# Bucket-sort ranks in a graph-network kernel: one scan and one predicated copy per bucket, with bucket totals from ScalarE

## The reference, cut to what matters

```
edge_index = jnp.stack([src, dst])
h = jnp.maximum(_layernorm(x, axis=-1), 0.0)
x = x + _L0_gnn_ref(h, edge_index, edge_weight1, ...)   # attention, segment_sum over dst
x = x + _L1_gnn_ref(h, edge_index, ...)                 # three rounds, segment_sum over dst and src
x = x + _L2_gnn_ref(h, edge_attr_256, edge_index, ...)  # softmax over dst and src together
x = x + _L3_gnn_ref(h, edge_index, edge_weight, ...)    # segment_sum over dst
```

## Time and profile before

| | us |
|---|---|
| median of three runs | 6442.14 |
| lowest, highest | 6439.19, 6449.53 |
| the profiled execution's own time | 6450.52 |
| its span, first to last instruction | 6448.7 |
| VectorE busy (share of the span) | 3708.4 (58%) |
| GpSimd busy | 3098.7 (48%) |
| TensorE busy | 3350.8 (52%) |
| ScalarE busy | 1198.0 (19%) |

### The profile page before, as it was taken

One profiled execution on the slowest core, in us unless ns is written; L12 is line 12 of the kernel. 1 busy time (PEld: TensorE's weight loads), 2 busy tenths in 40 slices (PEclk: granted clock), 3 DMA queues, 4 the chain that ended last, 5 costly groups with the idle time before them and its releaser, 6 DMA issues. The chain is left out here.

```text
span 6448.7 us, 88107 instructions
## 1 busy us (share of the span) xinstructions
PE 3350.8 (52%) x20820; PEld 2500.4 (39%) x20821; DVE 3708.4 (58%) x13503; ACT 1198.0 (19%) x3916; POOL 3098.7 (48%) x3167
## 2 busy tenths in 40 slices
PE   1000110016662666356638877968964988942333
PEld 0000010004442555345525544545554777732333
DVE  9200830049994777667777437337354888875444
ACT  0000000005551111011100000000003988930000
POOL 2777177726761777367730550541571000005775
PEclk9999999988886555555558888878987999975555
DMA  7000000006662333243327677657742434401112
GB/s 291 3 3 3 22 3 3 3 12 175 191 185 85 78 77 77 28 84 78 77 45 134 140 156 136 151 131 144 170 110 59 114 100 119 114 23 47 49 50 45
DMA packets 942678, 567.18 MB, mean 88 GB/s; under 512 B 598770, under 2 KB 873436, under 8 KB 938460
## 3 DMA queue, kind: packets, MB, share of 16 engines
q1 hardware_dynamic: 841820, 405.86, 24.7%
q0 software_dynamic: 100608, 158.42, 11.6%
HBM read 384.62 MB, written 179.43 MB: 87 GB/s over the span
## 5 line engine op out<-in xcount | busy, mean ns | idle before, releaser
L796 POOL DMA_INDIRECT fild_g<-table,fild_ring x416 | 427.6, 1028 | 1102.5 <-ACT fild_ring L810 978.7
L235 POOL DMA_INDIRECT recordsS<-sortS_rS,sortS_addrS x416 | 425.4, 1023 | 262.9 <-DVE sortS_addrS L276 136.5
L796 POOL DMA_INDIRECT gatAp_g<-table_heads,gatAp_ring x416 | 429.3, 1032 | 246.3 <-issue 123.7
L796 POOL DMA_INDIRECT gatBp_g<-table_head,gatBp_ring x416 | 411.6, 990 | 237.8 <-issue 122.8
L235 POOL DMA_INDIRECT recordsD<-sortD_rD,sortD_addrD x392 | 401.1, 1023 | 221.8 <-issue 119.1
L860 PE MATMUL fild_ps<-fild_g,fild_oh 128*128 128x128 f32 x832 | 213.2, 438 | 396.0 <-DMA fild_g<-table,fild_ring 267.4
L756 PE MATMUL pairs_p_b<-pairs_blk,pairs_oh 128*128 128x256 f16 x1024 | 294.1, 313 | 177.0 <-DVE pairs_oh L743 134.7
L860 PEld LDWEIGHTS fild_ps<-fild_g,fild_oh 128*128 128x128 f32 x832 | 185.2, 327 | 423.9 <-DVE fild_oh L912 198.0
L154 POOL DMA_INDIRECT gcn0e_held_attr<-in_edge_attr,recD x184 | 178.8, 971 | 354.1 <-POOLq L86 262.2
L771 ACT CAST pairs_blk<-pairs_p_b 128x512 f16<-128x512 f32 x512 | 285.2, 587 | 219.0 <-PE pairs_p_b L758 160.8
L154 POOL DMA_INDIRECT gcn2e_held_attr<-in_edge_attr,indexS x184 | 178.9, 972 | 281.2 <-POOLq L86 189.5
(11 more groups left out here) (656 smaller groups left out, 10465.5 us busy)
## 6 DMA issues: line engine op xcount, KB each, us to landing
gcnw_strip<-pairs SPq DMA_DIRECT2D x150, 800.0 KB, 6.5
pairs<-pairs_blk SPq DMA_DIRECT2D x768, 64.0 KB
pairs<-sortD_blank SPq DMA_DIRECT2D x27, 1600.0 KB, 38.0
attD_g<-attrD SPq DMA_DIRECT2D x104, 256.0 KB, 3.6
attS_g<-attrS SPq DMA_DIRECT2D x104, 256.0 KB, 3.6
pairs<-pairs_blk POOLq DMA_DIRECT2D x256, 64.0 KB, 2.3
attrD<-pairs_held_attr SPq DMA_DIRECT2D x56, 256.0 KB, 2.5
gatAp_rowb<-locD SPq DMA_DIRECT2D x104, 128.0 KB, 3.0
```

The costliest lines, as they stand in the source:

```text
L235: pool.indirect_dma_start(self.rec_dram, bass.IndirectOffsetOnAxis(ap=self.addr[:, c:c + 1], axis=0), self.r[:, c, :], None, bounds_check= ...
L796: pool.indirect_dma_start(rows(u, k), None, table, bass.IndirectOffsetOnAxis(ap=ring[:, u, k:k + 1], axis=0)).then_inc(gathered[u], 16)
```

## The change

The bucket totals are made first. ScalarE copies each one-hot plane and sums it along the columns into `tot` (`totals`); TensorE adds these sums over the partitions with a matrix of ones (`p_tot`), between buckets 3 and 4; the seven small instructions follow at once. Then TensorE makes one row per bucket instead of two: two matmuls into the same PSUM buffer give the increment from one column's rank to the next, `before` of this column plus `after` (ones minus `before`) of the column ahead of it. VectorE sums that row along the columns, with the bucket's first slot as the starting value, and copies the result into `slot` where the plane is one. There are four PSUM buffers for the rows instead of two. One GpSimd instruction makes `after16`. The stages behind are the same.

```
+            link(nc.gpsimd.tensor_tensor(C.after16[:], C.ones[:], C.before[:], ALU.subtract))
...
-        self.p_w = [ph.ps(f"p_w{side}{q}", [P, 512]) for q in range(2)]
-        self.p_t = [ph.ps(f"p_t{side}{q}", [P, 512]) for q in range(2)]
+        self.p_w = [ph.ps(f"p_w{side}{q}", [P, 512]) for q in range(4)]
+        self.p_tot = ph.ps("p_tot" + side, [P, NT])
+        self.junk = sb("junk", [P, 2, ncol], BF16)
...
+    def totals(self, act):
+        for b in range(NT):
+            act.wait_ge(self.oh_made, b + 1)
+            if b >= 2:
+                act.wait_ge(self.totalled, b - 1)
+            self.nc.scalar.activation(self.junk[:, b % 2], self.ohb[:, b, :], ACT.Copy,
+                                      accum_out=self.tot[:, b:b + 1]).then_inc(self.totalled, 1)
+
     def rank(self, V, dve):
...
+        dve.wait_ge(self.summed_up, 1)
+        V.ts(self.first[:], self.p_tot[:], float(P - 1), ALU.add)
...
         for b in range(NT):
             dve.wait_ge(self.ranked, b + 1)
-            V.link(nc.vector.tensor_tensor_scan(self.cum[:, 1:n + 1], self.p_t[b % 2][:, 0:n], self.zero[:], 0.0, ALU.add, ALU.add))
-            nc.vector.tensor_copy(self.tot[:, b:b + 1], self.cum[:, n:n + 1])
-            nc.vector.tensor_tensor(self.tmp[:], self.cum[:, 0:n], self.p_w[b % 2][:, 0:n], ALU.add).then_inc(self.taken, 1)
+            nc.vector.tensor_tensor_scan(self.cum[:, 0:n], self.p_w[b % 4][:, 0:n], self.zero[:],
+                                         self.first128[:, b:b + 1], ALU.add, ALU.add).then_inc(self.taken, 1)
             dve.wait_ge(self.taken, b + 1)
-            V.tt(self.tmp[:], self.tmp[:], self.ohb[:, b, :], ALU.mult)
-            V.tt(self.slot[:], self.slot[:], self.tmp[:], ALU.add)
...
-        for b in range(NT):
-            V.stt(self.slot[:], self.ohb[:, b, :], self.first128[:, b:b + 1], self.slot[:], ALU.mult, ALU.add)
+            V.link(nc.vector.copy_predicated(self.slot[:], self.ohb[:, b, :].bitcast(dt.uint16), self.cum[:, 0:n]))
...
             pe.wait_ge(self.oh_made, b + 1)
-            if b >= 2:
-                pe.wait_ge(self.taken, b - 1)
-            nc.tensor.matmul(self.p_w[b % 2][:, 0:n], self.C.before16[:], self.ohb[:, b, :], start=True, stop=True)
-            nc.tensor.matmul(self.p_t[b % 2][:, 0:n], self.C.ones16[:], self.ohb[:, b, :], start=True, stop=True).then_inc(self.ranked, 1)
+            if b == 4:
+                pe.wait_ge(self.totalled, NT)
+                nc.tensor.matmul(self.p_tot[:], self.C.ones[:], self.tot[:], start=True, stop=True).then_inc(self.summed_up, 1)
+            if b >= 4:
+                pe.wait_ge(self.taken, b - 3)
+            nc.tensor.matmul(self.p_w[b % 4][:, 0:n], self.C.before16[:], self.ohb[:, b, :], start=True, stop=False)
+            nc.tensor.matmul(self.p_w[b % 4][:, 1:n], self.C.after16[:], self.ohb[:, b, 0:n - 1], start=False,
+                             stop=True).then_inc(self.ranked, 1)
...
+        @block.scalar
+        def _(act):
+            j.totals(act)
```

More of the change, by code:

```diff
@@ L205, in __init__ @@
         self.first = sb("first", [P, NT])
+        self.tiles = sb("tiles", [P, NT])
         self.first128 = sb("first128", [P, NT])
-        self.p_w = [ph.ps(f"p_w{side}{q}", [P, 512]) for q in range(2)]
-        self.p_t = [ph.ps(f"p_t{side}{q}", [P, 512]) for q in range(2)]
+        self.p_w = [ph.ps(f"p_w{side}{q}", [P, 512]) for q in range(4)]
+        self.p_tot = ph.ps("p_tot" + side, [P, NT])
+        self.junk = sb("junk", [P, 2, ncol], BF16)
+        self.totalled, self.summed_up = ph.sem("totalled" + side), ph.sem("summed_up" + side)
         self.p_cnt = ph.ps("p_cnt" + side, [P, NT])
@@ L250, in rank @@
             nc.vector.tensor_scalar(self.ohb[:, b, :], self.bucketf[:], float(b), None, ALU.is_equal).then_inc(self.oh_made, 1)
+        dve.wait_ge(self.summed_up, 1)
+        V.ts(self.first[:], self.p_tot[:], float(P - 1), ALU.add)
+        V.link(nc.vector.tensor_copy(self.toti[:], self.first[:]))
+        V.link(nc.vector.tensor_single_scalar(self.toti[:], self.toti[:], P.bit_length() - 1, ALU.logical_shift_right))
+        V.link(nc.vector.tensor_copy(self.tiles[:], self.toti[:]))
+        V.link(nc.vector.tensor_tensor_scan(self.first[:], self.tiles[:], self.zero[:, 0:NT], 0.0, ALU.add, ALU.add))
@@ L251, in rank @@
+        V.tt(self.first[:], self.first[:], self.tiles[:], ALU.subtract)
+        V.ts(self.first128[:], self.first[:], float(P), ALU.mult)
         for b in range(NT):
             dve.wait_ge(self.ranked, b + 1)
-            V.link(nc.vector.tensor_tensor_scan(self.cum[:, 1:n + 1], self.p_t[b % 2][:, 0:n], self.zero[:], 0.0, ALU.add, ALU.add))
-            nc.vector.tensor_copy(self.tot[:, b:b + 1], self.cum[:, n:n + 1])
-            nc.vector.tensor_tensor(self.tmp[:], self.cum[:, 0:n], self.p_w[b % 2][:, 0:n], ALU.add).then_inc(self.taken, 1)
+            nc.vector.tensor_tensor_scan(self.cum[:, 0:n], self.p_w[b % 4][:, 0:n], self.zero[:],
+                                         self.first128[:, b:b + 1], ALU.add, ALU.add).then_inc(self.taken, 1)
@@ L263, in rank @@
-        V.link(nc.vector.tensor_tensor_scan(self.first[:], self.tot[:], self.zero[:, 0:NT], 0.0, ALU.add, ALU.add))
-        V.tt(self.first[:], self.first[:], self.tot[:], ALU.subtract)
-        V.ts(self.first128[:], self.first[:], float(P), ALU.mult)
-        for b in range(NT):
-            V.stt(self.slot[:], self.ohb[:, b, :], self.first128[:, b:b + 1], self.slot[:], ALU.mult, ALU.add)
+            V.link(nc.vector.copy_predicated(self.slot[:], self.ohb[:, b, :].bitcast(dt.uint16), self.cum[:, 0:n]))
@@ L2217, in program @@
         C.before16 = sb("before16", [P, P], BF16)
+        C.after16 = sb("after16", [P, P], BF16)
         C.ext_col = sb("ext_col", [1, NE], I32)
```

## The result

After the change the kernel takes 6435.18 us (median of 17 runs, 6430.63 to 6441.06), beside 6446.54 for the kernel before in the same comparison: a ratio of 0.9984 (95% interval 0.9976 to 0.9991). That is a gain of 11 us where 71 were forecast. The profile after was taken on an execution with a span of 6439.2 us.

A forecast was written before the change was run, and what follows sets the result against it. VectorE's ranking followed by GpSimd's scatters, twice, was taken to bound the sorts. Gains of 34.1 us in D and 36.9 in S, less 0.4, made 71: 6371 us against 6442.1, with 6354 to 6394 holding about 8 in 10.

The forecast's parts named there:

- A microsecond off the ranking should therefore be one off the kernel.: Both sorts: GpSimd's scatters wait for VectorE's ranking, 89.80 us in D and 93.57 in S, so its savings carry through whole.
- The passes behind `addr` are unchanged and move with it.: Behind each sort's address cast: the passes keep their length and start earlier by the gain; no cost counted.
- The sum: Whole kernel: 34.1 us gained in D plus 36.9 in S, less 0.4 for constants, 71 us rounded.
- the sign to look for: Stages behind the sorts: one that runs longer than before would show what the sum left out.
- The bucket loop: VectorE's 25 buckets per sort: 1.71 us each in D and 1.79 in S, together 42.7 and 44.7 us.
- The totals: ScalarE's 25 plane sums per sort, ahead of VectorE's loop: 0.63 us each in D, 0.65 in S.
- ScalarE's table load: Start of D's totals on ScalarE: 1.28 us charged to sort D, none in S.
- The overlap in that price: ScalarE's pitch per total: each copy in a row was taken to overlap its neighbour by about 0.07 us.
- ScalarE or VectorE: Place of the totals: VectorE alone would expose 14 us instead of 11, some 3 us a sort worse.
- The scatters beside the blank stores: GpSimd's earlier D scatters while blank stores fill the DMA engines: costed at nothing.
- The first rival: Sort D: scatters stand behind the blank stores, so D gains nothing and the kernel takes 6405; chance 8%.
- the other two: Sorts' ranking: predicated copy slow, 6461 at 2.4 us each, 3%; or ScalarE's totals so late nothing is gained, 6442, 2%.

The follow-up runs named there:

- run 6: Kernel after with 9 one-column memsets on VectorE in sort D behind the low compare, moving its later loops 8 instructions: 6364.89 us, ratio 0.9881.
- run 9: Kernel after with each bucket's predicated copy replaced by multiplication and addition, the rest of the change kept, loops lying well: 6396.23 us.
- run 7: Kernel after with all 25 bucket totals reduced by VectorE and none summed by ScalarE, no memsets: 6382.17 us.
- run 8: Kernel after with ScalarE summing 18 bucket totals and VectorE reducing 7, no memsets: 6356.89 us, ratio 0.9870.
- run 2: Kernel after with 129 one-column memsets on VectorE in sort D behind the low compare, moving its later loops 128 instructions: 6436.60 us.
- run 4: Kernel after with 24 memsets on GpSimd ahead of sort D's scatters to start them later, VectorE's program untouched: 6487.33 us.

## Why the prediction was wrong

**The step that failed** is the end of the first paragraph: "A microsecond off the ranking should therefore be one off the kernel." It puts everything behind the ranking at nothing, as does "The passes behind `addr` are unchanged and move with it." The code of the later stages is unchanged and the barriers do carry a gain on, but VectorE's program for them had moved by 198 instructions. Of the 78 us that the sorts gained, the attention D loop took back 66 and gather B 6. The sum had no term for it, the rivals no case, and no row of the kernel before showed a loop that pays. The text did name the sign to look for, a later stage that runs longer.

**The sum itself stood.** With the loops lying well the kernel takes 6364.89 (run 6) where 6371 was forecast, inside the range; the gain is 80 us beside 71. Point by point:
- *The bucket loop*: forecast 42.7 and 44.7 us; in D from 39.01 to 81.50, 42.5. The scan's start value costs 0.06 as the earlier trace rows had it (1.03 against 0.97), the predicated copy with the 16-bit mask 0.60 as taken from the 32-bit one, and run 9 confirms what it is worth.
- *The totals* were mis-sized: 0.51 us each, not 0.63, since reading out a sum (0.18) lies beside the next pass. Over 25 that is 3 us a sort. ScalarE's table load, charged to D with 1.28, came at 4.9 us while ScalarE was idle. Together they make the 4 us by which D beat its 34.1; S, with 40.2 against 36.9, had the 3 alone. The overlap in that price was misread too: four copies overlap three times, so the row gives 0.10 us and not 0.07.
- *ScalarE or VectorE*: the forecast put VectorE-only some 3 us a sort behind, and in D it was 5.3 (run 7). The Trainium skill ("ScalarE: Activation LUTs", Rules for kernel authors) would give adds to VectorE. The traces agree only that a sum of a plane is a little shorter there, 0.47 against 0.51. But VectorE is the engine that the sort waits for, and in run 8, where each took a part, the sorts were done soonest.
- *The scatters beside the blank stores*: nothing, as costed. They start at 86.43, and their mean stayed 1023 ns. The first rival didn't happen, nor did the other two.

**Why the same stall costs 66 us in one loop and 6 in another.** After the change VectorE's waits on "issue" are 63.1 us in attention D and 55.7 us in gather B (of the first line here, a wait for gathered rows, there were 128.7 us before):

```profile
DVE gatBp_z L1016 <- DMA gatBp_g<-table_head,gatBp_ring: 84.6, 58, 4.6
DVE gatBp_msg L1051 <- issue: 29.6, 10, 3.4
DVE gatB_acc L1040 <- issue: 26.1, 12, 2.7
```

In gather B VectorE waits for gathered rows anyway, and the stall comes out of that wait: 44 us of it went. GpSimd's 416 gathers set that pass, with 417.2 us of work and 118.8 of issue. Attention D has no such slack. Before, ScalarE was busy 321.3 us and TensorE 318.4 of its 352.5, and by the waits above both wait for VectorE's `attD_df` once it stands still. TensorE's clock falls after the stall (windows of the turn shown above: busy us of PE, PEld, DVE, ACT, POOL, then granted clock, DMA share, GB/s):

```profile
4941.00:4949.00 8.00, 4.25 (x34) 3.57 (x33) 1.48 (x7) 3.77 (x13) 0.00 (x0) 0.98 0.47 132
4949.00:4957.00 8.00, 5.34 (x31) 5.37 (x32) 6.06 (x35) 4.50 (x16) 0.00 (x0) 0.59 0.00 1
```

After eight microseconds in which TensorE was busy for 4.25, the granted clock is 0.59 of full, mostly the 1.2 GHz level instead of 2.4, and full again in the 23 us behind. What that adds to the price no run separates from the stall.

The Trainium skill ("Runtime: NRT & Kernel Launch", Instruction fetch mechanics) says that a taken branch whose target is no longer held forces a fetch before execution goes on; the traces agree, with 4 to 7 us a turn. It gives the blocks as 256 instructions, two of them held; here the measurements decide otherwise, since run 2, moved by 128, paid just as much.

## What to carry to other kernels

A change that adds or removes instructions moves every loop behind it on that engine, and here a loop of 274 instructions paid or not by where it began. So compare the length of every later stage before believing a total, and read the instruction queue's packet count: if it rises while the code behind is the same, shift the loop with a few idle instructions and time again. And a stall is worth what the engine's slack leaves of it: the same 55 to 63 us were nearly free where VectorE waited for gathers, and cost all of it where three engines hand work round.

## What was not expected of the hardware

GpSimd's scatter takes 0.97 us alone, as from 157.71 us on, when VectorE is done with the low compare. Beside the compare it takes 1.63 (timelines of GpSimd and of VectorE, after):

```profile
101.61 1.07 POOL L239 DMA_INDIRECT recordsD<-sortD_rD,sortD_addrD  x1 [0.30 <-issue]
102.98 2.17 POOL L239 DMA_INDIRECT recordsD<-sortD_rD,sortD_addrD  x1 [0.30 <-issue]
105.45 1.63 POOL L239 DMA_INDIRECT recordsD<-sortD_rD,sortD_addrD  x1 [0.30 <-issue]
107.39 1.63 POOL L239 DMA_INDIRECT recordsD<-sortD_rD,sortD_addrD  x1 [0.31 <-issue]
```
```profile
102.28 54.28 DVE L296 TENSOR_TENSOR sortD_lowD<-iota_row,sortD_locfD 128x1792 bf16<-128x1792 f32 x28
```

The step at 102.98 is where VectorE's compare begins. The blank stores are not its cause: in the kernel before the same step comes at 140.95, with the stores done. From then on a scatter starts every 1.94 us, and a compare takes 54.28/28 = 1.94: one scatter gets through per compare. In run 4 the scatters began as the compare was ending, and took 981 ns in the mean instead of 1023: 16.5 us of sort D, lost in both kernels alike, that another place for the compare might win. That was not tried. The Trainium skill ("SBUF — State Buffer", SBUF: two separate sides) says that VectorE, in some of its operations, locks GpSimd out of a port that it needs to write a transfer's descriptors, and that such a lock is held for a whole instruction. One scatter per compare agrees with that; that the port is the cause no run shows.
